# Set-up of the second attention: order of its transfers, of its first statistics and of its column sums, and the way of the first q pieces into the stacks

## What is computed

```python
x = x + moe(layernorm(x))                          # top 2 experts of 8 for each token
q = split_heads(layernorm(x) @ Wq.T + bq)          # 16 heads of 16
k, v = split_heads(ctx @ Wk.T + bk), split_heads(ctx @ Wv.T + bv)
scores = einsum('bhqd,bhkd->bhqk', q, k) / sqrt(16)
scores = where(mask == 0, -1e9, scores)
x = x + merge(softmax(scores) @ v) @ Wo.T + bo
x = x + routed_attention(layernorm(x))
```

## Time and profile before

| | us |
|---|---|
| median of 3 runs | 2191.31 |
| range of the 3 runs | 2186.43 to 2195.64 |
| the profiled execution | 2194.6 |
| its span, first to last instruction | 2192.8 |
| mean granted TensorE clock of the span | 0.939 |
| PE / DVE / ACT / POOL busy, of the span | 88% / 60% / 41% / 41% |

### The profile page before, as it was taken

How to read it: one execution, slowest core, us unless ns; L and a number is a source line. 1 busy time by engine, 2 the same in 40 slices (tenths; PEclk the granted TensorE clock), 3 DMA queues, 4 the chain that set the end, 5 groups by cost and what they waited for, 6 DMA issues and landing times. The chain is left out here.

```text
span 2192.8 us, 37227 instructions
## 1 busy us (share of the span) xinstructions
PE 1935.3 (88%) x11503; PEld 1366.9 (62%) x11512; DVE 1323.2 (60%) x2280; ACT 909.3 (41%) x1548; POOL 908.6 (41%) x869
## 2 busy tenths in 40 slices
PE   4882799999999996389999999848999999999997
PEld 2682799999999996133333333345666666665664
DVE  6873444545545544488899888665555555555554
ACT  4631233333333333046676666542333333334332
POOL 0047633633633601345555333552444444344433
PEclk9955899999999998679999999968999999999999
DMA  6555323233233223534544443334444344434432
GB/s 224 202 185 198 114 72 129 78 124 129 72 129 129 72 72 107 135 124 136 136 130 131 116 115 113 92 114 142 109 107 93 94 107 97 102 93 117 97 84 73
DMA packets 159623, 257.53 MB, mean 117 GB/s; under 512 B 26054, under 2 KB 78358, under 8 KB 156242
## 3 DMA queue, kind: packets, MB, share of 16 engines
q1 hardware_dynamic: 114218, 176.24, 29.1%
q0 software_dynamic: 15536, 43.55, 6.2%
q10 hardware_dynamic: 29816, 37.08, 5.4%
HBM read 128.87 MB, written 71.11 MB: 91 GB/s over the span
## 5 line engine op out<-in xcount | busy, mean ns | idle before, releaser
L1326 DVE TENSOR_REDUCE ca_negmax<-ca_na 128x2 f32<-128x1024 f32 x272 | 330.9, 1220 | 43.3 <-PE ca_na L1026 40.2
L1164 ACT ACTIVATE ca_pr<-ca_st 128x512 f32<-128x512 f32 x512 | 279.2, 600 | 138.1 <-PE ca_st L1040 136.7
L758 DVE TENSOR_TENSOR ex_h<-ex_up,ex_sg 128x512 f32<-128x512 f32 x136 | 94.0, 692 | 305.5 <-ACT ex_sg L721 198.9
L2006 DVE TENSOR_REDUCE sa_negmax<-sa_na 128x1 f32<-128x512 f32 x272 | 176.2, 679 | 117.2 <-PE sa_na L1677 117.0
L1026 PE MATMUL ca_na<-ca_k_stack,ca_q_stack 64*128 64x512 f32 x544 | 214.1, 472 | 14.3 <-DMA ca_q_stack<-cross_q 8.0
L681 PE MATMUL ex_gp<-ex_xp,moe_gu_p 128*128 128x256 f32 x1632 | 222.3, 286 | 1.7 <-DVE ex_xp L744 1.4
L1040 PE MATMUL ca_st<-ca_q_stack,ca_k_stack 64*128 64x512 f32 x512 | 207.2, 465 | 17.6 <-ACT ca_pr L1164 17.0
L694 PE MATMUL ex_yp<-moe_dn_p,ex_hp 128*128 128x256 f32 x1632 | 209.3, 286 | 12.4 <-DVE ex_hp L748 12.4
L681 PE MATMUL ex_up<-ex_xp,moe_gu_p 128*128 128x256 f32 x1632 | 218.1, 283 | 0.0
L694 PEld LDWEIGHTS ex_yp<-moe_dn_p,ex_hp 128*128 128x128 f32 x1632 | 198.8, 191 | 16.7 <-DVE ex_hp L748 16.7
L681 PEld LDWEIGHTS ex_gp<-ex_xp,moe_gu_p 128*128 128x128 f32 x1632 | 206.0, 192 | 3.2 <-DVE ex_xp L744 1.8
(11 more groups left out here) (332 smaller groups left out, 3526.9 us busy)
## 6 DMA issues: line engine op xcount, KB each, us to landing
ex_raw_m<-masks ACTq DMA_DIRECT2D x34, 512.0 KB, 3.8
sa_q<-sa_qh SPq DMA_DIRECT2D x136, 128.0 KB
sa_k<-sa_kh SPq DMA_DIRECT2D x136, 128.0 KB
ca_q_stack<-cross_q SPq DMA_DIRECT2D x216, 64.0 KB
ca_k_stack<-cross_k SPq DMA_DIRECT2D x204, 64.0 KB
moe_gu_raw<-gateupT POOLq DMA_DIRECT2D x6, 2048.0 KB, 8.2
cross_q<-ca_qp SPq DMA_DIRECT2D x9, 1024.0 KB, 5.1
mask_bias<-ex_made ACTq DMA_DIRECT2D x35, 256.0 KB, 2.4
```

The source lines that it names most:

```text
L1164: act.activation(pr[:, s // HG % 2, s % HG, :], st[s % 2][:, :], ACT.Exp, scale=DK ** -0.5).then_inc(exp_done, 1)
L1326: dve.tensor_reduce(negmax[:, g % 2, 1 - r % 2, :, r // 2], na[r % 2][:, :, :], AX.X, ALU.max, negate=True).then_inc(max_done, 1)
L2006: dve.tensor_reduce(negmax[:, par, h, t:t + 1], na[s % 2][:, :], AX.X, ALU.max, negate=True).then_inc(max_done, 1)
```

## The change

The transposed mask bias of batch 0, wq and bq are loaded first; SP and ACT load the k stacks only once batch 0 is gathered, and bv, bo, wo and the other mask bias come behind them. "rv" of batch 0 is the first job. Batch 0 is weighted and measured tile by tile, each tile with a semaphore of its own. POOL issues the gathers of batch 1 behind the first root. DVE evacuates q before it needs bv, bo and wo. The first q pieces go from `qp` straight into the stacks, 48 transfers of 32 KB instead of 24 of 64 KB; SP sends those of i = 0 and ACT those of i = 1. The store of each half to DRAM stays, behind its pieces. The loop itself is as it was.

```diff
-        FIRST = [("xT0", 0, None), ("xT1", 0, None), ("rv", 0, None), ("q0", 0, None), ("q1", 0, None), ("bo", 0, 0), ...
+        FIRST = [("rv", 0, None), ("xT0", 0, None), ("xT1", 0, None), ("q0", 0, None), ("q1", 0, None), ("bo", 0, 0), ...
...
+        def send_q(queue, g, i):
+            for j in range(2):
+                src = g % 2 * HG * DK + (2 * i + j) * DK
+                for r in range(3):
+                    lo = j * HALF + r * DK
+                    queue.dma_start(q_stack[g][lo:lo + DK, i, :].bitcast(F32), qp[src:src + DK, r % 2, g // 2, :].bitcast(F32)).then_inc(stack_in[g], 16)
...
-            for name in ("wq", "wo"):
-                sp.dma_start(weights[name]...).then_inc(w_in, 16)
-            for name in ("bq", "bv"):
-                sp.dma_start(weights[name]...).then_inc(w_in, 16)
-            sp.dma_start(bo[:, :], ...).then_inc(w_in, 16)
             load_bias_T(0, 0)
-            load_bias(0, 0)
+            sp.dma_start(wq[:, :, :], ...).then_inc(wq_in, 16)
+            sp.dma_start(bq[:, :], ...).then_inc(wq_in, 16)
             sp.wait_ge(set_up, SETUP)
+            sp.wait_ge(tile_in[TB - 1], 16 * TOPK)
             for g in range(2):
                 load_k(g, 0)
+            (bv, bo, wo: the same transfers, on w_in)
+            load_bias(0, 0)
             for c in range(KC):
+                sp.wait_ge(qp_ready, c + 1)
+                for g in range(2 * c, 2 * c + 2):
+                    send_q(sp, g, 0)
                 store_half(c)
-                sp.wait_ge(half_stored[c], 16)
-                for g in range(2 * c, 2 * c + 2):
-                    load_q(g, 0)
             load_bias_T(1, 1)
...
-            pe.wait_ge(w_in, 16 * 5)
             pe.wait_ge(set_up, SETUP)
             for n, (name, b, spot) in enumerate(FIRST):
                 if spot is None:
+                    if name == "q0":
+                        pe.wait_ge(wq_in, 32)
                     prepare(n, name, b)
             pe.wait_ge(set_late, 3)
             for t in range(TB - 1):
                 values(G - 1, t)
+            pe.wait_ge(w_in, 16 * 3)
...
             act.wait_ge(set_up, SETUP)
+            act.wait_ge(tile_in[TB - 1], 16 * TOPK)
             for g in range(2, G):
                 load_k(g)
-            act.wait_ge(w_in, 16 * 5)
             (evacuate xT0, xT1 of batch 0)
+            for g in range(G):
+                if g % 2 == 0:
+                    act.wait_ge(qp_ready, g // 2 + 1)
+                send_q(act, g, 1)
             (evacuate the other "x" and "m" jobs)
...
-            for b in range(2):
-                for tile in range(TB):
-                    gather(b, tile, b)
+            for tile in range(TB):
+                gather(0, tile, tile_in[tile], 0)
             pool.wait_ge(wk_set, 2)
             root(0)
+            for tile in range(TB):
+                gather(1, tile, gathered[1], 1)
             for c in range(KC):
                 split_q(c, first(f"q{c}", 0), 0)
...
-            for step in range(4):
-                absorb(0, step, range(TB), 0, 16 * TOPK * TB)
+            evacuate(0, "rv", 0, None, None)
+            for tile in range(TB):
+                for step in range(4):
+                    absorb(0, step, (tile,), 0, 16 * TOPK, tile_in[tile], 6)
             deviation(0)
             normalise(0, 0)
-            dve.wait_ge(w_in, 16 * 5)
+            dve.wait_ge(wq_in, 32)
+            (evacuate q0, q1)
+            dve.wait_ge(w_in, 16 * 3)
             for c in range(KC):
                 dve.tensor_copy(bvb[:, c, :], ...).then_inc(bvb_ready, 1)
-            (evacuate rv, q0, q1)
             for step in range(4):
                 absorb(1, step, range(TB), 1, 16 * TOPK * TB)
```

More of the change, by code:

```diff
@@ L1190, in split_q @@
                         pool.wait_ge(half_stored[c], 16)
+                        for g in range(2 * c, 2 * c + 2):
+                            pool.wait_ge(stack_in[g], LOAD0)
                 else:
@@ L1236, in _ @@
             for tile in range(TB):
-                gather(2, tile, 0)
+                gather(2, tile, gathered[0], 0)
             pool.wait_ge(set_late, 3)
@@ L1288, in absorb @@
                             dve.wait_ge(first_in, t + 1)
+                        elif done is not None:
+                            dve.wait_ge(done, count)
                         elif tile == 0:
```

45 lines of the change are left out of this document (25 added, 20 removed).

## The result

The kernel after takes 2185.85 us (median of 20 runs, 2180.63 to 2191.63), the kernel before 2191.26 in the same sitting (20 runs, 2186.43 to 2198.39). The ratio is 0.9976, 95% interval 0.9967 to 0.9984: 5.4 us, with bounds of 3.5 and 7.2, where 15.5 had been forecast. That is within 0.5%, which the prediction had given 0.19. The stated range (2167 to 2186) still holds 2185.85, by 0.15 us; that is luck, since only a third of the forecast gain came. The profiled execution took 2185.81 us, its span is 2184.1 at a mean clock of 0.937. Shares of the span have hardly moved: the first two lines are the page's busy times and its clock row.

What follows compares the result with a forecast made beforehand. The prediction took the set-up before the second attention's loop, about 90 us, as paid in full; its steps put run 6 15.5 us earlier, so 2191.3 - 15.5 = 2175.8 us, range 2167 to 2186.

Steps and rivals of the forecast that it cites:

- Parts 1, 2 and 4: Set-up: batch 0's rows 5.75 us earlier; column sums off the path, q0 8.45 earlier; DVE's list, first maximum 8.35 earlier.
- Part 2's other bound: q1 in the set-up: PE still at the lower clock costs about 1.8 us once; 0 was kept.
- Part 5: Runs 0 to 5 of the first scores: 8.89 us as before, change 0, bounds -1.4 and +1.
- part 3: q pieces without DRAM: six issues per queue in 3.1 us plus 2.2, stack full at 902.6, 13.2 us earlier.
- part 6: Wait for batch 1's mask bias before run 6: bias landed at 915.8, run 6 at 919.45, 15.5 us earlier.
- rival C: q pieces issue slowly, 1.13 us each: run 6 only 2.3 us earlier, 2189; chance 0.07 without loss, 0.05 with loss.
- A: Batch 1's gathers land late, batch 1 begins 4.7 us late: gain 10.8, 2180.5 us; chance 0.13.
- B: PE enters the loop at the high clock, up to 5.5 us less in its first 12 us: 2171; chance 0.13.
- D: Batch 0's last gather still lands at 883, so only 2.7 + 7 us go: about 2181.5; chance 0.05.

Runs made afterwards that it cites:

- e2: Kernel after with q going through DRAM and back by SP alone, as before the change, instead of direct pieces: 2238.57 us, ratio 0.9968.
- e5: Kernel after with q through DRAM and batch 1's mask bias issued behind the first half's loads: 2178.02 us, ratio 0.9940.
- e1_both_moved: Kernel after with batch 1's mask bias behind SP's first 12 pieces and ACT's copy ahead of its second 12: 2232.57 us, ratio 0.9941.
- e3: Kernel after with all 48 q pieces sent by SP and none by ACT: 2251.65 us, ratio 1.0024.
- before_again: Kernel before, unchanged, in a single run for a second trace: 2188.95 us.
- e7: Kernel after without the two waits that hold the k stacks back until batch 0 is gathered: 2185.03 us, ratio 0.9963.
- e6: Kernel after with batch 0 weighted step by step over its tiles, still with a semaphore per tile: 2182.49 us, ratio 0.9952.
- e1b_bias_moved: Kernel after with only batch 1's mask bias moved behind SP's first 12 pieces, ACT's list unchanged: 2181.46 us, ratio 0.9960.
- e1_repeat: The kernel of e1_both_moved (direct pieces, mask bias and ACT's copy moved) run again on another chip: 2181.91 us, ratio 0.9946.
- e9: Kernel after with q through DRAM, mask bias behind the first half's loads, batch 0 step by step over tiles: 2178.21 us, ratio 0.9928.
- after_again: Kernel after, unchanged, run once more for a second trace: 2237.03 us, ratio 0.9961.

## Why the prediction was wrong in its size

Both profiled executions begin the set-up at the same time (863.62 and 863.58), so the prediction's times can be read straight against those of the trace.

| step of the prediction | forecast | trace |
|---|---|---|
| 1: first addition, no wait | 875.8 | 875.47 |
| 1: statistics of batch 0 end | 882.4 | 881.88 |
| 1: normalised rows ready | 886.3 | 885.62 |
| 2: q0 starts | 890.05 | 889.41 |
| 2: first half split; q1 evacuated | 897.3; 897.45 | 896.71; 898.55 |
| 3: stack full, first scores | 902.6 | 903.69 |
| 4: batch 1 begins; first maximum | 898.2; 908.7 | 898.74; 909.66 |
| 5: run 5 ends | 917.6 | 920.97 |
| 3, 6: mask bias issued | 910.7 | 915.94 |
| 6: mask bias landed | 915.8 | 922.73 |
| 6: run 6 | 919.45 | 925.78 |
| loop's first scores | 938 | 944.81 |

**Parts 1, 2 and 4 held,** each within 1.1 us. The serial tiles took 6.41 (6.6 taken, with 5.2 and 8.6 as bounds). The landing of the last gather, taken as 3.0 to 4.6 from a row that mixes batches, was 2.7; no row of batch 0 in the trace of before lies under 5.0, so that this term came out is in part luck. DVE and no transfer is late at the first maximum; e2 shows it from the other side. The Trainium skill (SBUF — State Buffer, Who interferes with whom) has POOL shut out by a tensor_scalar in a two-port mode, which is what the prediction feared for the normalising beside the gathers. Nothing of the kind is seen here: the gathers that lie in it began at 883.55 and 884.88, 1.33 apart against 1.25 later on (the first two of batch 0, with no normalising beside them, stand 1.36 apart: 864.32 and 865.68), and the four instructions took 1.44 against 1.38 in the earlier trace rows. Neither side lost more than 0.1 us. In which mode they ran no trace shows.

**Part 2's other bound came true:** q1 ran at the low level, four matmuls in 3.69 (894.08; granted clock 0.52 from 894.2 to 897.7), where the same four took 1.98 in e5 (897.05; 1.00 from 897.1 to 899.0). The choice of 0 was wrong by 1.7 us at PE. At the first maximum DVE is 1.0 late, since q0 was 0.6 early and the copies of bv took 0.2 instead of 0.7, while batch 1 took 11.0 instead of 10.45.

**Part 5 went past its bound:** runs 0 to 5 took 11.31 (909.66 to 920.97) instead of 8.89 + 1 at most. That is ACT's late copy again, 1.97 us in their middle: in e1_both_moved, with the copy moved, they take 9.28. It cost nothing more here, since the bias came later still.

**The step that failed is the price of a piece,** in part 3, which part 6 multiplies by 24. It was taken as 0.52, from loads of 64 KB out of DRAM; the argument against rival C was that 32 KB is less than the 128 KB of the earlier trace rows. Those same rows had a nearer price: the zero row `zrow` also lies in SBUF, the memory on the chip, and its transfer into a q stack took 0.65 us to issue though it is only 8 KB (877.75). With the 0.04 between two issues that makes 24 x 0.69 = 16.6 us, and the bias would have been forecast at 914.8. The trace gives 0.81 in SP's first half, 0.68 in its second, and 18.9 us for ACT's 24 (896.74 to 915.67), 0.79. The bytes alone do not set it: e3 has 0.64 to 0.69 for a piece with one queue sending, about as much as the 8 KB of `zrow`, while loads of 64 KB out of DRAM took 0.45 to 0.63 in the traces here. Whether the source, the rows or the layout makes a piece dear was not tried. In part 3 the error is hidden (1.1 us late, under DVE's list, as the prediction said it would be). In part 6 it is not: SP's 24 took 9.75 + 8.11 = 17.9 us instead of 12.5, and the bias was issued 5.24 late. To that come 1.7 us of landing, 6.8 instead of 5.1. This is the stretch 916 to 923 us of the kernel after (length; busy us and instructions of PE, PEld, DVE, ACT, POOL; clock, DMA share, GB/s):

```profile
916.00:923.00 7.00, 2.54 (x9) 1.36 (x10) 2.36 (x2) 0.84 (x2) 1.39 (x3) 0.50 0.94 283
```

The DMA engines are nearly full there, but they were so before too (0.89 from 926.50 to 931.64), so the load doesn't explain the longer landing. In the other traces in which PE waits for this bias it took 5.1 (e3), 5.8 (e2), 6.1 (before_again), 6.4 (e7) and 7.8 (e6); why is open.

5.24 + 1.69, less 0.6 of slack that the sum had at this place (landed 915.8, PE free 916.4), is the 6.33 by which run 6 was missed. The moved transfer of e1b_bias_moved confirms the first term, and e1_both_moved the copy that stands behind it. The prediction named rival C for this, worked it out for 1.13 us a piece, and gave it 0.12. What it lacked was the case between: no stall at the first scores, and still two lists that end 5 us late. Its own bound for the landing was a single value, and its own test ("part 3 wrong if pieces stand more than 0.7 apart, part 6 if PE waits for the bias or ACT's copy") fired on both counts.

The Trainium skill (DMA: Bandwidth & Descriptors, Issuing engines are not separate DMA queues) says that issuing on several engines at once only saves the time of initiating a DMA, "which is usually small relative to the DMA itself". For a stack of such pieces it is the larger part here: from the first issue to the first scores it is 6.95 us (896.74 to 903.69), of which six issues of 0.81 on each queue are 4.9. The Trainium skill (Perfetto Trace Analysis, DMA Instruction — HWDGE (DVE, Sync)) says that the time shown for an issue holds a wait for the descriptor generator, which is locked for exclusive use. If SP and ACT shared one such lock for the whole of an issue, two queues together would be no faster than one. They are faster: one queue alone puts out a piece each 0.64 to 0.69 us (e3), both together one each 0.39 (48 in 18.9 us). How much of the time is a wait for the other, no trace here shows.

**From the set-up to the time.** The loop begins 8.9 us earlier and the span ends 8.7 earlier, so nothing was given back behind the set-up. The medians say 5.4. That difference is the execution the prediction worked from, which stood 3.3 us above its median, while the one of the kernel after stood on its own (2185.81 and 2185.85). The prediction took the same 15.5 off both, as if those 3.3 us lay outside the set-up. About 1.8 of them may lie in it: its set-up was 90.1 us long, the other trace of the same kernel has 88.3. Where the rest lies is open; the second sitting gave 9.6.

**Rivals.** A (late gathers of batch 1) fell: DVE went from the copies of bv to batch 1 at 898.74 with no wait. B (PE comes in at the high clock) did not come: the loop's first stretch still ran near the low level, 0.52 in this row of the kernel after, against 0.50 in the earlier trace rows. A stall of 4.15 us was left there, but where none is left the first 12 us have 0.52 (e1_both_moved), 0.54 (e1_repeat) and 0.57 (e9) too. Only e1b has 0.78, and what raised it is not known.

```profile
944.00:956.00 12.00, 11.59 (x42) 4.27 (x43) 9.52 (x22) 5.17 (x10) 7.46 (x14) 0.52 0.89 297
```

D (the last gather still late) fell with the landings. C holds in kind: the 0.81 lies midway between the 0.52 of the sum and C's 1.13.

**What stays open.** q0 and q1 stood in the same order behind the same work of PE in all kernels with the change, and q1 found the low clock in after, after_again, e1_both_moved, e1_repeat, e1b, e7 and e9, the high one in e2, e3, e5 and e6. No edit separates the two sets, and the kernel before has it both ways (q1 evacuated 2.8 us behind q0 in one trace, 4.6 in the other). No run was made to settle it. It is worth 1.7 us, and may be part of what scatters the set-ups of one kernel. Which of the transfers moved back behind the k stacks frees the gathers is open as well.

## What to carry to other kernels

When transfers are cut into more and smaller ones, count instructions per queue, price one from a row of the same kind (source, rows, queue) even if its size is another, and follow everything behind them in both issuing lists, also what an engine like ACT has to compute there. Look first at who is queued behind whom: one load moved ahead of transfers that were needed later gave a gain that can't be told from that of the whole change. A transfer made faster than the engine that waits beside it gives nothing, so ask what is late next before paying for it elsewhere.

## What the runs showed of the hardware

- Issuing a transfer of 32 KB between SBUF partitions (16 rows) took 0.64 to 0.69 us on one queue (e3, and the second half in e1_both_moved), 0.68 to 0.85 with a second queue at the same work (kernel after, e1b); 8 KB between SBUF partitions took 0.65, 64 KB from DRAM 0.45 (e2, second half) to 0.63 (before_again). The two queues together put out more than one (a piece each 0.39 us), so splitting the pieces is worth it even though each gets dearer: without it the set-up was 11.8 us longer (e3).
- Batch 0's indirect gathers land in 2.7 us at the median (4.5 at most) with only three loads issued beside them, in 5.0 (6.8) with the k stacks beside them (e7), and in 7.8 (9.9) with all loads and sixteen gathers under way, in the kernel before.
- The mask bias took 6.8 us from issue to use in both traces of the changed kernel, against 5.1 before and in e3 (943.44 to 948.50), at a DMA share of 0.93, 0.89 and 0.90 from issue to use.
- ACT did not compute while it issued: its 0.58 us copy stood behind 24 issues, and the trace gives "issue" as the releaser and names no semaphore (915.67). PE waited 1.97 us for it in the kernel after, 2.6 in e1b and 3.1 in e6.
